# Two pairs of maxima made before the first scores, and one weight piece issued behind the rows of the third group of heads

## What is computed

```python
x = x + a_alpha * attention(gamma * rmsnorm(x) + beta)     # 16 heads of 16 features
x = x + f_alpha * (silu(n @ gate.T) * (n @ hidden.T) @ out_w.T + out_b)   # n = ada_rmsnorm(x), 1024 hidden
out = (layernorm(x) * w + bias + tanh(cond @ lin_w.T + lin_b)) * w + bias

# attention, per batch and head
p = softmax(scale * q @ k.T, axis=-1)
o = p @ v
```

## Time and profile before

| | |
|---|---|
| median of three runs | 759.37 us (758.07 to 760.06) |
| the profiled execution | 758.38 us, of which 756.5 us is the span |
| mean granted TensorE clock | 0.988 of full speed |
| PE busy | 717.1 us, 95% |
| DVE busy | 535.0 us, 71% |
| ACT busy | 470.2 us, 62% |
| POOL busy | 392.3 us, 52% |

### The profile page before, as it was taken

The page is one execution under the profiler, slowest core; times in us unless marked ns, Lnnn a source line. Parts: engine busy times, 40 slices in busy tenths (PEclk is TensorE's granted clock), DMA queues, the critical chain, the costliest instruction groups (busy, mean ns, idle before and its releaser), DMA issues.

```text
span 756.5 us, 17527 instructions
## 1 busy us (share of the span) xinstructions
PE 717.1 (95%) x6660; PEld 490.3 (65%) x6660; DVE 535.0 (71%) x797; ACT 470.2 (62%) x860; POOL 392.3 (52%) x493
## 2 busy tenths in 40 slices
PE   6698999999999999999999999999999999999995
PEld 5343444557767677766777567766676667678895
DVE  4787787786776877777676867767677776436765
ACT  4467777785666676675666756676566665743431
POOL 4364243543386625746376644846257444872533
PEclk9889999999999999999999999999999999999998
DMA  7577657464424544354434544265343530232110
GB/s 228 168 226 243 204 168 270 125 220 137 156 58 166 191 151 137 106 200 153 141 114 140 182 144 161 61 196 151 126 155 119 186 108 3 75 105 64 49 52 29
DMA packets 63276, 107.18 MB, mean 142 GB/s; under 512 B 10480, under 2 KB 18344, under 8 KB 63192
## 3 DMA queue, kind: packets, MB, share of 16 engines
q1 hardware_dynamic: 61892, 104.66, 43.6%
q10 hardware_dynamic: 1172, 1.20, 0.6%
q0 software_dynamic: 128, 0.20, 0.1%
HBM read 57.50 MB, written 37.52 MB: 126 GB/s over the span
## 4 chain that ended last, share of the span: by engine, by line
PE 71%; DVE 10%; issue 6%; DMA 5%; ACT 3%; POOL 2%; SPq 1%; ACTq 0%; POOLq 0%; DVEq 0%
PE ps_x L1438 17%; PE ps_o L1411 12%; PE ps_j L1309 11%; PE ps_j L1451 10%; PE ps_s L1398 8%; PE ps_m L1379 6%; DVE mx L1127 3%; PE ps_o L1451 2%; DVE fx L1093 2%; ACT prob L922 2%; DVE gate_t L1167 2%; DMA d_c<-reciprocal_scratch 1%; DMA reciprocal_scratch<-d_s 1%; PE ps_m L1438 1%; PE ps_s L1438 1%
## 5 line engine op out<-in xcount | busy, mean ns | idle before, releaser
L1127 DVE TENSOR_REDUCE mx<-ps_m 128x2 f32<-128x1024 f32 x212 | 259.5, 1224 | 115.4 <-PE ps_m L1379 114.8
L922 ACT ACTIVATE prob<-ps_s 128x1024 f32<-128x1024 f32 x218 | 223.1, 1023 | 56.1 <-PE ps_s L1398 53.9
L1411 PE MATMUL ps_o<-prob,v 128*32 128x512 f32 x1024 | 137.2, 608 | 0.3 <-ACT o_raw L930 0.2
L1398 PEld LDWEIGHTS ps_s<-qs,ks 64*128 64x128 f32 x436 | 41.0, 184 | 99.4 <-issue 77.1
L1398 PE MATMUL ps_s<-qs,ks 64*128 64x512 f32 x436 | 99.8, 454 | 4.7 <-issue 3.8
L1438 PE MATMUL ps_x<-n,gh_hi 64*128 64x256 f32 x872 | 97.7, 284 | 1.7 <-DVE act_y L1174 1.6
L635 POOL TENSOR_TENSOR a_lo<-act_y,a_hi 128x256 fp32r<-128x256 f32 x100 | 73.7, 737 | 45.3 <-ACT a_hi L953 45.1
L1379 PE MATMUL ps_m<-ks,qs 64*128 64x512 f32 x424 | 88.6, 413 | 7.6 <-DVE mx L1127 3.9
L1438 PE MATMUL ps_x<-n_x,gh_hi 64*128 64x256 f32 x872 | 94.4, 276 | 0.0
L660 POOL TENSOR_TENSOR xr<-xr,sc 128x512 f32<-128x512 f32 x41 | 53.3, 1299 | 59.3 <-DVE sc L1139 40.5
L1438 PEld LDWEIGHTS ps_x<-n,gh_hi 64*128 64x128 f32 x872 | 74.2, 184 | 13.7 <-DVE act_y L1174 10.2
(11 more groups left out here) (191 smaller groups left out, 1524.4 us busy)
## 6 DMA issues: line engine op xcount, KB each, us to landing
qs<-stack_scratch SPq DMA_DIRECT2D x30, 512.0 KB, 4.5
ks<-stack_scratch SPq DMA_DIRECT2D x30, 512.0 KB, 6.2
stack_scratch<-qk_hi SPq DMA_DIRECT2D x56, 256.0 KB, 3.2
out_scratch<-o_raw SPq DMA_DIRECT2D x32, 256.0 KB, 3.7
n_x<-n SPq DMA_DIRECT2D x32, 256.0 KB, 3.7
stack_scratch<-qk_lo SPq DMA_DIRECT2D x28, 256.0 KB, 3.3
on_lo<-out_scratch SPq DMA_DIRECT2D x16, 256.0 KB
d_c<-reciprocal_scratch SPq DMA_DIRECT2D x16, 256.0 KB
```

Of the source, the lines that this page charges most:

```text
L922: act.activation(prob[:, n % 2, 2 * h:2 * h + 2, :], score_pair(n, h)[:], ACT.Exp, scale=SCALE).then_inc(p_r, 1)
L1127: dve.tensor_reduce(mx[:, group % 2, :, h, qt], max_pair(mp)[:], AX.X, ALU.max).then_inc(mx_red, 1)
L1398: mm = pe.matmul(score_pair(n, j)[:, s, :], ks[r:r + 64, g, j, kb * P:(kb + 1) * P], qs[r:r + 64, g, j, :], start=True, stop=True)
L1411: mm = pe.matmul(ps_o[32 * i:32 * i + 32, :], v[:, g, kb, i, :], prob[:, n % 2, i, :], start=(kb == 0), stop=(kb == TT - 1), skip_group_ch ...
```

## The change

The number of pairs ahead of unit 0 goes from 10 to 12. Unit 0 makes pair 12 alone where it made 10, 11 and 12; unit 1 keeps 13, 14 and 15. SP issues piece 7 in unit 6 instead of unit 5, behind `max_rows(0, 2)`.

```diff
-LEAD_IN = 10
+LEAD_IN = 12
...
         def early_maxima(n):
 
             if n < 2:
-                return range(LEAD_IN + 3 * n, LEAD_IN + 3 * n + 3)
+                return range(LEAD_IN + n, LEAD_IN + 3 * n + 1)
             return range(2 * (n + LEAD), 2 * (n + LEAD) + 2)
...
                 for w in range(4, PIECES):
-                    if n == max(PIECE_AT[w - 4], 2):
+                    if n == max(PIECE_AT[w - 4], 2) + (PIECE_AT[w - 4] == 5):
                         load_piece(w)
```

## The result

The changed kernel takes 760.58 us (median of 21 executions, 757.64 to 764.85), the kernel before, run beside it, 758.07 us (21, 756.68 to 760.18). The ratio is 1.0029 with a 95% interval of 1.0016 to 1.0042, some 2.2 us slower: inside the stated range, at the edge of the 0.3% taken as "no change", and ten times the 0.2 us of the sum. What stands out is the spread: the slowest execution of the changed kernel is 4.7 us above the slowest of before.

The account below looks back on a forecast made before the run. PE was taken as the bound, busy 19.75 of 20 us from 80 us on. 0 at the start, -0.91 at unit 8 and +0.91 + 0.24 at unit 10 gave +0.2 us: 759.6 us as a median, range 757.3 to 761.4.

Parts of the forecast that it names:

- the stated range: Whole kernel: 757.3 to 761.4 us around a forecast of 759.6, with 0.89 chance of being within 0.3%.
- the sum: Whole kernel: 0 at the start, -0.91 us at unit 8, +0.91 + 0.24 at unit 10, together +0.2 us.
- rival C: Units 0 and 1: clock returns later as two pairs leave; 0.50 over 46 to 48 us, 1.7 us, 761.3; chance 0.10.
- Part 1, where the pairs go: Ahead of S(0,0): M(10) and M(11) run from about 33.8 to 35.7 us, inside PE's gap, 0.8 us before the rows.
- Part 1, its price of 0: Unit 0: TR(1,1) still starts at 40.48, behind about 1 us of idle PE; PE's cost and gain 0, DVE's price 0.
- The clock's rule: Start of the kernel: the skill warns a long idle gap between matmul bursts takes the engine back to half its clock.
- rival B: Units 0 and 1: clock stays up or returns sooner, saving 3.2 us, to 756.4 us; chance 0.05.
- Part 2 at unit 8: S(8,0) starts 0.56 to 0.91 us earlier as the third group's rows go ahead of piece 7; 0.91 taken.
- Part 2 at unit 10: M(32) waits for the read into `ks`, issued 0.24 us later; unit 8's 0.91 us is waited away and 0.24 lost.
- after the same 6.8 us: Unit 10: the read into `ks`, issued at 68.46, takes 6.8 us as before and lands at 75.26.
- rival D: Unit 10: piece 7's 0.82 us of data all go ahead of `ks`, M(32) 0.82 us later still, 760.4 us; chance 0.07.
- Rival A: Unit 10: the read into `ks` doesn't hold M(32), so unit 8's 0.91 us is kept, 758.5 us; chance 0.08.

Follow-up runs that it names:

- e9: Repeat of e1: against the kernel before, only the 12 pairs ahead of unit 0, piece 7 left in unit 5; 759.24 us, ratio 1.0009.
- e7: The changed kernel run once more, unaltered, against the kernel before; 761.60 us (6 executions), ratio 1.0040.
- e3: The changed kernel plus two unread 128x512 matmuls in unit 0 between S(0,1) and the transposes; 758.46 us, ratio 0.9996 to the kernel before.
- e11: e10 plus two unread matmuls in unit 0, as in e3; 757.08 us, ratio 0.9979 to the kernel before.
- e10: The changed kernel with pieces 7 and 8 both issued in unit 7, behind stack_read(1, 0); 758.89 us, ratio 0.9997 to the kernel before.
- e5: The kernel before, with M(11) and M(12) looking at only the first 128 keys; 759.19 us, ratio 1.0013.
- e6: The kernel before plus unread matmuls ahead of unit 0: two behind each of M(5) to M(8), ten behind M(9); 760.85 us, ratio 1.0025.
- e1: Against the kernel before: only the 12 pairs of maxima ahead of unit 0, piece 7 left in unit 5; 759.39 us, ratio 1.0023.
- e2: Against the kernel before: only piece 7 moved behind the third group's rows, 10 pairs ahead of unit 0; 759.38 us, ratio 1.0006.
- e8: The kernel before with e6's unread matmuls, and pieces 7 and 8 issued in unit 7 behind stack_read(1, 0); 760.07 us, ratio 1.0019.

## Why the prediction was right, and where it was not

The time lies in the range, but that is the range's merit, which took in rival C, and not the sum's: the sum has +0.2 us, the runs +2.2 and +3.0. A small slip besides: the clock's mean of 0.73 over 44 to 46 us means 1.08 us at half and 0.92 at full speed, not the other way round; the rise at 45.1 is right.

**Part 1, where the pairs go: right.** Both pairs lie in the gap, M(11) ends before the rows come, TR(1,1) starts behind 0.99 us of idle PE and behind the same chain of copies, and DVE hides its two reductions.

**Part 1, its price of 0: the term that was mis-sized.** I wrote "so TR(1,1) still starts at 40.48, behind about 1 us of idle PE instead of behind two pairs: gain 0". That idle time isn't free. It stood in the text as rival C with a chance of 0.10 and a granted clock of 0.50 over 46 to 48 us as its mark. No profile shows that mark in full: the first has 1.00 there, e9 0.84, e7 0.64 with the rise at 47.4. So C is no case beside the forecast: it seems to happen, more or less, in a share of the executions, and moves their mean. Its size by the profiles is 0.8 us up to S(2,0); by executions the 12 pairs alone measure 1.0023 and 1.0009, together some 1.2 us. I had priced it at 1.7. That it is PE's missing work is shown by the times: e3 against the changed kernel, e11 against e10, and in sign e5. That it acts through the clock is argued: e11's profile (rise 3.7 us behind S(0,0), where e10 has 7.7) and the mean clocks speak for it, e3's profile doesn't, and it is a matter of averages, not of every execution.

**The clock's rule: not borne out in the direction of rival B.** Filling the gap with the two pairs did not keep the clock up (0.57 over 32 to 34 us), as the rows of before said. But the Trainium skill ("TensorE: Matmul & The Clock Gate", "Why this matters for your kernels") names sustained busy time as what brings the full clock, and that half of it the prediction has in rival C alone: the change takes PE's work from the very stretch in which the clock returns. The averages of the table agree (6.2 us with the two pairs in place, 8.4 without). e6's profile doesn't: there PE is busy in every stretch from 26 us on, and the clock is down until about 38. So the rule alone doesn't tell when the clock returns here, and the measurements decide.

**Part 2 at unit 8: right.** The idle at S(8,0) fell from 1.50 to 0.37 us, the rows went out in one piece, and S(8,0) stands 3.31 us behind the third group's transposition instead of 4.43: 1.1 us earlier, a little more than the 0.56 to 0.91 forecast.

**Part 2 at unit 10: the mechanism right, two sizes off.** M(32) waits for the read into `ks`, as forecast, and on average what unit 8 won is given back: 0.0 us between the two averages of T3 to M(32). The read is issued 0.8 us later, not 0.24, since the idle 0.45 us moved on to the pieces instead of vanishing. To land it takes 5.5, 6.1, 6.3 and 6.9 us in the four profiles that have piece 7 ahead of it and behind the rows, and 5.4, 6.8 and 7.2 in the three with the old order (e9, before, e1), so the assumption "after the same 6.8 us" had no ground. These rows don't show rival D either: piece 7 doesn't make the landing longer. Rival A (the gain is kept) came in part in the first profile, whose M(32) stands 0.58 us earlier than before (10.41 against 10.99), and not in e7 (11.74).

**What no part of the prediction had:** the waits at S(8,0) and M(32), 1.50 and 0.75 us, became 0.36 to 0.39 and 1.00 to 2.36 us, and behind the two longest of the four the clock fell again. The price is 1.2 us at S(11,0) in e7 and 0.9 in e2. How often this happens, the executions without a profile don't tell.

**The sum.** Part 1 measures about +1.2 us, part 2 +0.5 us by its ratio with an interval from -0.8 to +1.6, both together +2.2 and +3.0. The parts alone are less than the whole, within their intervals. That the rest is the falls in unit 10 is likely but not shown: e10, which has the 12 pairs and no wait for the read, comes back to 0.9997. What remains open is how much of the executions above 762 us (5 of 21) comes from a late DMA or a fall near the end of the kernel, as e8 shows them; no profile of the changed kernel has either. Open, too, is why keeping the clock up (e6, e8) brought no time, and with it how much of part 1's price the clock explains.

## What to carry to other kernels

Before idle time of a busy engine is called free, ask what clock it is running at: at the lower clock, work that looks hidden may be what brings the full clock back, and moving it out of that stretch can cost more than the wait it fills. When a transfer is moved ahead of another, follow the queue to the next consumer that is within a microsecond of being late; here the reads ahead of both pieces kept the gain that the rows alone only moved. A kernel whose median moves little but whose slowest executions move by 4 us has a cause that one profile may miss; repeat it until a slow execution is the profiled one.

## What the runs showed that was not expected

Useful work removed made the kernel slower (e5, +0.13%, just clear of the noise), and useless work added made it faster (e3 against the changed kernel, 0.9996 against 1.0029). But the same means overdone cost time (e6): ten unread matmuls took 3.89 us at half clock where e8 shows 2.6 us at full clock. And one write that landed 2 us late near the end (e8) lengthened a wait of PE to 3.71 us, behind which the clock fell at about 695 us: 4 us in all, of which the fall is some 1.6.
